# Eight batches of attention and FFN on one core: the last rotation, the block sums, the last contexts and bn_aggr moved

## The reference

```python
q = _rmsnorm(q_in @ wq_a.T) ; q = (q @ wq_b.T)          # 384 latent columns, 16 heads of 128 + 64
kv = x @ wkv_a.T ; kv_c = _rmsnorm(kv[..., :128])       # 128 latent columns, 64 rotated ones shared by heads
scores = einsum(qf, kf) * SCALE ; attn = softmax(scores) # 512 x 512 for each head
out = einsum(attn, v) ; x = x + out @ wo.T
x = x + down((silu(LN(x) @ gate) * (LN(x) @ up)))       # 512 -> 1536 -> 512
```

## Time and profile before

| what | us |
|---|---|
| median of three runs | 2216.45 |
| lowest and highest run | 2216.08, 2217.67 |
| the profiled execution, its own time | 2217.94 |
| its span | 2216.1 |
| PE busy | 2183.9 |
| DVE busy | 1595.4 |
| POOL busy | 1361.4 |
| ACT busy | 1281.6 |

### The profile page before, as it was taken

The page is one execution under the profiler, slowest core; times in us unless marked ns, Lnnn a source line. Parts: engine busy times, 40 slices in busy tenths (PEclk is TensorE's granted clock), DMA queues, the critical chain, the costliest instruction groups (busy, mean ns, idle before and its releaser), DMA issues.

```text
span 2216.1 us, 37420 instructions
## 1 busy us (share of the span) xinstructions
PE 2183.9 (99%) x11732; PEld 1100.9 (50%) x11732; DVE 1595.4 (72%) x3581; ACT 1281.6 (58%) x2688; POOL 1361.4 (61%) x1083
## 2 busy tenths in 40 slices
PE   7999999999999999999999999999999999999999
PEld 5444544445445564455644555445654556445554
DVE  7888886877567775777767777677766777467773
ACT  6666564554377732877328763487434874367722
POOL 4657466785378833887249772588536874368732
PEclk9999999999999999999999999999999999999999
DMA  7868436775158841788318882188723896148730
GB/s 247 190 124 151 91 72 149 153 149 119 29 127 160 163 96 22 147 163 167 77 32 158 164 155 65 41 169 161 142 55 64 167 165 127 27 98 157 148 82 20
DMA packets 734362, 265.44 MB, mean 120 GB/s; under 512 B 687312, under 2 KB 703696, under 8 KB 733136
## 3 DMA queue, kind: packets, MB, share of 16 engines
q1 hardware_dynamic: 734160, 263.05, 57.6%
HBM read 79.31 MB, written 14.81 MB: 42 GB/s over the span
## 4 chain that ended last, share of the span: by engine, by line
PE 85%; DVE 7%; POOL 2%; DMA 2%; ACT 2%; SPq 1%; issue 1%; DVEq 0%; ACTq 0%; POOLq 0%
PE bank L1108 13%; PE bank L921 8%; PE scores L1118 7%; PE bank L349 6%; PE bank L351 6%; PE bank L350 6%; PE scores L813 5%; PE scores L351 5%; PE scores L350 5%; PE scores L349 5%; PE bank L832 4%; PE bank L834 4%; PE bank L833 4%; PE scores L810 3%; DVE arena L1803 2%
## 5 line engine op out<-in xcount | busy, mean ns | idle before, releaser
L1774 DVE TENSOR_REDUCE mx<-scores 128x1 f32<-128x512 f32 x512 | 353.3, 690 | 62.7 <-PE scores L351 62.3
L2306 POOL TENSOR_TENSOR arena<-arena 128x1024 f16<-128x1024 f32 x168 | 354.3, 2131 | 38.2 <-ACT arena L1365 38.2
L1349 ACT ACTIVATE arena<-scores,shift 128x512 f32<-128x512 f32 x336 | 229.6, 686 | 148.5 <-DVE shift L1776 104.6
L1108 PE MATMUL bank<-arena,WFF 128*128 128x512 f16 x1392 | 313.5, 379 | 0.8 <-DVE arena L2099 0.6
L1858 DVE SCALAR_TENSOR_TENSOR arena<-bank,arena 128x512 f32<-128x512 f32 x336 | 216.8, 687 | 76.3 <-PE bank L921 75.5
L2405 POOL TENSOR_TENSOR arena<-arena 128x512 f16<-128x512 f32 x96 | 115.1, 1199 | 248.7 <-ACT arena L1491 248.7
L2221 POOL TENSOR_TENSOR arena<-arena 128x1024 f16<-128x1024 f32 x88 | 187.7, 2138 | 95.6 <-ACT arena L1339 95.4
L1108 PEld LDWEIGHTS bank<-arena,WFF 128*128 128x128 f16 x1392 | 136.0, 98 | 164.1 <-DVE arena L2099 2.3
L921 PE MATMUL bank<-WVO 128*128 128x256 f16 x1764 | 213.5, 273 | 0.3 <-DVE arena L1858 0.3
L813 PE MATMUL scores<-arena 128*128 128x512 f16 x512 | 195.4, 382 | 0.0
L921 PEld LDWEIGHTS bank<-WVO 128*128 128x128 f16 x1764 | 172.1, 98 | 46.1 <-DVE arena L1858 1.3
(11 more groups left out here) (198 smaller groups left out, 4699.8 us busy)
## 6 DMA issues: line engine op xcount, KB each, us to landing
WVO<-w_duo SPq DMA_DIRECT2D x42, 512.0 KB, 4.4
WVO<-w_duo SPq DMA_DIRECT2D x42, 384.0 KB, 3.9
arena<-arena SPq DMA_TRANSPOSE x712, 3.3
arena<-w_ffn SPq DMA_DIRECT2D x24, 384.0 KB, 3.5
arena<-x SPq DMA_DIRECT2D x8, 1024.0 KB, 5.7
out<-arena SPq DMA_DIRECT2D x32, 256.0 KB, 2.0
arena<-x SPq DMA_DIRECT2D x14, 512.0 KB, 4.6
WVO<-w_o SPq DMA_DIRECT2D x4, 1024.0 KB, 8.4
```

The lines of the kernel that those rows point to most:

```text
L1108: m = pe.matmul(dst[:, :], lhsT=w[:, c, k, :], rhs=XT[:, p, k, :], start=(k == 0 and p == 0), stop=(k == NK - 1 and p == 1))
L1774: dve.tensor_reduce(mx[:, t:t + 1], SC[:, t, :], AX_X, ALU.max).then_inc(s["mxr"], 1)
L2306: pool.tensor_tensor(PL[:, par, two, :], exps(i)[:, two, :], PH[:, par, two, :], ALU.subtract).then_inc(s["pl"], 1)
```

## The change

- **Rotation 7.** In batches 0 and 1 PE issues it behind scores(1), DVE takes it up behind the maxima of head 1, and in batch 1 POOL's part follows accordingly.
- **Transposes of head 0.** SP issues hi0, hi1, lo0, lo1 instead of hi0, lo0, hi1, lo1, in plain and duo batches.
- **Block sums (batch 1).** `block_sums(j, 0)` makes the first six steps in the even head, `block_sums(j, 1)` the other four in the next one; the low halves, ACT's high halves and SP's sums of blocks come one head later, and the rows of the next batch in heads 7, 9 and 11.
- **The last contexts.** For batches 1 to 7 ACT makes the high halves of the context of head 14 and of both halves of head 15 in the new `end_context_hi`, DVE only the low halves. `end_context_hi` waits for `outp` besides `ctp` and `cth`.
- **bn_aggr.** In batches 0 to 6 three of the four come between the third and the fourth bn_stats.
- **Batch 7.** The context of head 14 is one full operation, the second half's low part comes directly behind `stats(1)`, and `keep_warm(8)` becomes `keep_warm(4)`.

```diff
+        ROWS_PLAIN = {7: (0,), 9: (1, 2), 11: (3,)}
...
                 prob_rows_hi(g, par, 0)
+                if i == 0:
+                    prob_rows_hi(g, par, 1)
                 prob_rows_lo(g, par, 0)
-                prob_rows_hi(g, par, 1)
+                if i > 0:
+                    prob_rows_hi(g, par, 1)
                 prob_rows_lo(g, par, 1)
...
+                if i == 0:
+                    prob_rows_hi(b * NH, 0, 0)
+                    prob_rows_hi(b * NH, 0, 1)
+                    prob_rows_lo(b * NH, 0, 0)
+                    prob_rows_lo(b * NH, 0, 1)
+                    return
...
-                        if i >= 4 and i % 2 == 0:
-                            sums_of_blocks(i // 2 - 2)
+                        if i >= 5 and i % 2:
+                            sums_of_blocks((i - 5) // 2)
...
                 scores(b, pair, par)
+                if rot is not None:
+                    rotated_ahead(b, rot)
...
-                for n in range(rot_first(first) + 1, N_ROT):
-                    rotated_ahead(b, n)
+                    rotated_ahead(b, N_ROT - 1)
+                elif first:
+                    rotated_ahead(b, N_ROT - 2)
...
-                    head_step(b, 0, 1)
+                    head_step(b, 0, 1, rot=N_ROT - 1)
...
-                    keep_warm(8, SC[:, 2])
+                    keep_warm(4, SC[:, 2])
...
+            def end_context_hi(n, cols, src, read, parts=1):
+
+                act.wait_ge(s["ctp"], n + parts)
+                act.wait_ge(s["cth"], n)
+                act.wait_ge(s["outp"], read)
+                act.activation(CT[:, 0, cols], src[:, cols], ACT.Copy, scale=CS).then_inc(s["cth"], parts)
...
+                        if i >= 4 and i % 2 == 0:
+                            sum_hi(i // 2 - 2)
+                        for t in ROWS_PLAIN.get(i, ()):
+                            next_rows_hi(b, t)
...
+                    if plain and not first and k == 0:
+                        sum_hi(N_DUO - 2)
+                    if not first and k == 1:
+                        n, d = b * N_CT + 2 * N_DUO, order_of_head(b, 2 * N_DUO) if b >= B_PLAIN else (b * NH + NH - 2) * NT
+                        end_context_hi(n, slice(0, S), BQ, d, 2 if last else 1)
...
+                    for half in range(2):
+                        end_context_hi(n + 2 + half, half_cols(half), VBANK_END[1][half], d + 2 + 2 * half)
                     x_hi(b + 1)
                     return
-                for i in range(2, 2 * NT - 2):
+                latent(b + 1, 2)
+                if not first and plain:
+                    end_context_hi(n + 1, half_cols(0), VBANK_LAST[0], d + 2)
+                latent(b + 1, 3)
+                if not first and not plain:
+                    end_context_hi(n + 1, half_cols(0), VBANK_LATE[0], d + 2)
+                if not first:
+                    end_context_hi(n + 2, half_cols(1), (VBANK_LAST if plain else VBANK_LATE)[1], d + 4)
+                for i in range(4, 2 * NT - 2):
...
-            def context(n, cols, src=BC):
-
-                dve.wait_ge(s["ctp"], n + 1)
-                dve.tensor_scalar(CT[:, 0, cols], src[:, cols], CS, None, ALU.mult).then_inc(s["cth"], 1)
-                dve.wait_ge(s["cth"], n + 1)
-                split_lo(CT[:, 1, cols], src[:, cols], CS, CT[:, 0, cols]).then_inc(s["ctl"], 1)
+            def context(n, cols, src=BC, hi=True, parts=1):
+
+                if hi:
+                    dve.wait_ge(s["ctp"], n + 1)
+                    dve.tensor_scalar(CT[:, 0, cols], src[:, cols], CS, None, ALU.mult).then_inc(s["cth"], 1)
+                dve.wait_ge(s["cth"], n + parts)
+                split_lo(CT[:, 1, cols], src[:, cols], CS, CT[:, 0, cols]).then_inc(s["ctl"], parts)
...
+                if turned is not None:
+                    rot_products(b, turned, RBANK[turned % 2])
                 sums_of_head(g - 1, 1 - par)
+                if row is not None:
+                    next_rows(b, row)
...
-                dve.wait_ge(s["ctp"], n + 1)
-                for half in range(2):
-                    context(n - 1 + half, cols[half], BQ)
+                context(n - 1, slice(0, S), BQ, hi=False, parts=2)
...
                 stats(0)
                 stats(1)
+                context(n + 2, cols[1], VBANK_END[1][1], hi=False)
                 add_last(b, 7, 6)
-                context(n + 2, cols[1], VBANK_END[1][1])
                 norm(0)
...
-                context(n - 1, slice(0, S), BQ)
+                context(n - 1, slice(0, S), BQ, hi=first)
...
+                    if t == NT - 2:
+                        ch.wait()
+                        for k in range(NT - 1):
+                            ch.add(dve.bn_aggr(mv[:, k, :], bn[:, k, :]))
+                ch.add(dve.memset(rs_t[:, 0:NT], 0.0))
                 ch.wait()
-                ch.add(dve.memset(rs_t[:, 0:NT], 0.0))
-                for t in range(NT):
-                    ch.add(dve.bn_aggr(mv[:, t, :], bn[:, t, :]))
+                ch.add(dve.bn_aggr(mv[:, NT - 1, :], bn[:, NT - 1, :]))
...
+                if part == 1:
+                    step(t2, half(o, 0, 1), t1, ALU.subtract, 3)
+                    step(t2, t2, half(o, 1, 1), ALU.add, 7)
+                    step(t4, half(o, 0, 0), t2, ALU.subtract, 8)
+                    step(t4, t4, half(o, 1, 0), ALU.add, 9)
+                    return
...
-                step(t2, half(o, 0, 1), t1, ALU.subtract, 3)
-                step(t2, t2, half(o, 1, 1), ALU.add, 7)
-                step(t4, half(o, 0, 0), t2, ALU.subtract, 8)
-                step(t4, t4, half(o, 1, 0), ALU.add, 9)
...
-                        if i % 2 == 0:
-                            block_sums(i // 2 - 1)
-                        else:
-                            block_sums_lo(i // 2 - 1)
+                        j = i // 2 - 1
+                        if i % 2 == 0 and j > 0:
+                            block_sums_lo(j - 1)
+                        block_sums(j, i % 2)
...
+                if plain and not first:
+                    block_sums_lo(N_DUO - 1)
```

More of the change, by code:

```diff
@@ L300, in halves_landed, with half_cols @@
             return (b * (NH // 2) + i // 2) * 32
+        def half_cols(half):
+            return slice(2 * half * P, 2 * half * P + 2 * P)
         def any_bank(n):
@@ L597, in batch @@
                         next_input(b)
-                    if plain and i in (11, 12):
+                    if first and i in (11, 12):
                         turn_input(b, i - 11, stg)
+                    elif plain and i == 12:
+                        turn_input(b, 0, stg)
+                        turn_input(b, 1, stg)
                     if not plain and not last and i in TURN_STEPS:
@@ L978, in before, with head_step @@
                 return (pair, 0) if par else (pair - 1, 1)
-            def head_step(b, pair, par, first=False, ahead=True, weights=False):
+            def head_step(b, pair, par, first=False, ahead=True, weights=False, rot=None):
                 if weights:
@@ L1892, in duo_step, with head_step @@
                     duo_adds(b, (i - 5) // 2, (4, 5, 6, 7))
-            def head_step(i, b, par, ahead=True, chunk=None, part=None, weights=False, rot=None):
+            def head_step(i, b, par, ahead=True, chunk=None, part=None, weights=False, rot=None, turned=None, row=None):
                 g, n = b * NH + i, b * N_CT + i
@@ L1951, in attention @@
                     head_step(i, b, i % 2, chunk=chunk_of(i) if first else None, part=part,
-                              weights=first, rot=N_ROT - 1 if first and i == 2 else None)
-                    if not first and 7 <= i < 7 + NT:
-                        next_rows(b, i - 7)
+                              weights=first, rot=N_ROT - 1 if first and i == 2 else None,
+                              row=i - 7 if not first and 7 <= i < 7 + NT else None)
             def end_of_attention(b):
@@ L2004, in end_of_attention @@
                 duo_adds(b, N_DUO - 1, (0,))
-                context(n + 1, cols[0], VBANK_END[1][0])
+                context(n + 1, cols[0], VBANK_END[1][0], hi=False)
                 duo_adds(b, N_DUO - 1, (1, 2, 3))
@@ L2066, in last_of_attention @@
                 half_context = lambda half: context(n + half, slice(2 * half * P, 2 * half * P + 2 * P),
-                                                    (VBANK_LAST if b < B_PLAIN else VBANK_LATE)[half])
+                                                    (VBANK_LAST if b < B_PLAIN else VBANK_LATE)[half], hi=first)
                 if b >= B_PLAIN:
@@ L2254, in next_rows_lo, with block_sums @@
                 pool.tensor_tensor(STG[:, 1, t, :], XN[:, t, :], STG[:, 0, t, :], ALU.subtract).then_inc(s["xs"], 1)
-            def block_sums(j):
+            def block_sums(j, part):
                 k, e, o = 10 * j, WVO[:, 2 * j], WVO[:, 2 * j + 1]
@@ L2386, in attention @@
                         join_chunk(chunk_of(i - 1))
```

(12 more changed lines are left out.)

13 lines of the change are left out of this document (4 added, 9 removed).

## The result

The changed kernel takes 2223.68 us (median of eight runs, 2221.72 to 2225.64) against 2216.55 (eight runs, 2215.91 to 2217.67): ratio 1.0029, 95% interval 1.0020 to 1.0039. It is slower, by 4.4 to 8.6 us; 2217.4 had been forecast, with a range that ended at 2221.4. The forecast was 0.9 us above the median before; the measured step is 7.1. The profiled execution took 2222.42 us with a span of 2220.6, against 2217.94 and 2216.1 before, so the two traces explain 4.5 us.

What follows compares the result with a forecast made beforehand. PE, busy 99%, was taken as the bound, with some 11 us of waits to win. Terms +4.5, +1.5, -1.6, -1.6, -1.75 made +1.0 on 2217.94, so 2218.9, less 1.5 to the median: 2217.4, range 2211.8 to 2221.4.

Steps and rivals of the forecast that it cites:

- The gate: Head 14's context, batches 2 to 6: ACT's high half waits for `outp` after the sixth pair's products; +4.5 us in all.
- the slack: Before head 14's projection, batch 3: DVE's second add ended 1.11 us before PE needed it.
- next_rows: hidden: Next batch's rows, moved earlier in DVE heads 7 to 10 and POOL and ACT heads 7, 9, 11: 0 us.
- bn_aggr: Layer norm, batches 0 to 6: three aggregations ahead of the last bn_stats add one dependent drain; +0.2 us each, +1.5.
- Rival 2: Layer norm: early bn_aggr is free, since DVE holds the next operation anyway; -1.5 us, giving 2215.9; chance 0.13.
- Block sums: Batch 1: ten steps split over even and odd heads bring transposes sooner, removing PE's waits; -1.6 us.
- the order of the transposes: Head 0 of batches 2, 3 and 6: hi1 ahead of lo0 lands lo1 earlier, removing PE's waits; -1.6 us.
- The rotation: Rotation 7 behind scores(1), batches 0 and 1: the wait moves into the scores, values(0) starts as before; 0 us.
- Batch 7: Last batch: earlier projection and norm, four fewer warming products, second transposes earlier; -1.75 us.
- rival 4: Batch 7: clock still 0.50 at the transposes and gate products, up to 4.2 us more, 2221.6; chance 0.16.

Runs made afterwards that it cites:

- Experiment 2: Changed kernel, but in duo batches ACT's high half of head 14's context waits for `outp` only at the batch-start count: 2217.90 us, ratio 0.9999.
- experiment 7: Version of experiment 4 with the duo batches' `outp` wait set two counts below the full one: 2214.14 us, ratio 0.9984.
- Experiment 1: Changed kernel with DVE's next_rows of heads 7 to 10 of batch 1 behind the additions again: 2221.17 us, ratio 1.0014.
- experiment 5: Changed kernel with next_rows as scalar_tensor_tensor with a broadcast scale, at the same new place: 2224.59 us, ratio 1.0028.
- experiment 8: Kernel before plus only the two-part block sums, with their POOL, ACT and SP parts: 2216.42 us, ratio 0.9994.
- experiment 4: Changed kernel with three repairs: next_rows behind the additions, weak `outp` wait in duo batches, four bn_aggr together again: 2213.39 us, ratio 0.9980.
- experiment 6: Version of experiment 4 with the last rotation back ahead of head 1's scores in batches 0 and 1: 2213.02 us, ratio 0.9980.

## Why the prediction was wrong

Its sum was +1.0 us on the profiled execution; the traces say +4.5, the medians +7.1.

**The gate was right in place and nearly in size.** Forecast +0.8 and +0.1 a batch, measured 0.88 and 0.20; the additions 1.93 us later were 1.86 later, and the second addition was what PE waited for. Experiment 2 takes it away, experiment 7 finds no price inside the slack. What was mis-sized is the last batch: +0.2 was named for the gate there, and left out of the sum, and 1.1 came back when it was weakened.

**The step that failed is "next_rows: hidden".** I reasoned that DVE is busy 72% of the span and waits for PE before each context, took the operation to be as short at the new place as elsewhere, and gave it 0 us. It cost 2.23, in three waits of 0.72 to 0.77. Two things were missed. The new place is, within some hundredths of a us, the moment at which POOL starts the split of a head's probabilities, since both follow ACT's last exponential. And this DVE operation, when it begins while POOL works, ends 0.28 us behind the end of an operation of POOL: so in all nine of its executions of this kind in the trace before and in all seven after. The trace of before already showed it, where the wait was covered; POOL, then DVE:

```profile
458.42 2.13 POOL L2286 TENSOR_TENSOR WVO<-arena,WVO 128x1024 f16<-128x1024 f32 x1
...
458.59 0.68 DVE L1562 SCALAR_TENSOR_TENSOR arena<-bank,arena 128x512 f16<-128x512 f32 x1
459.19 1.65 DVE L1676 TENSOR_SCALAR arena<-arena,mv,rs_x 128x512 f32<-128x512 f32 x1
```

Inside POOL's 2.13 us an operation that reads a bank took its usual 0.68 us; the row operation behind it, which reads and writes float32 in SBUF, began at 459.19 and ended at 460.84, 0.29 behind POOL's end. In the trace before, the four executions in heads 7 to 10 of batch 1 took 1.05, 1.00, 1.65 and 0.79 us: all four were held, where it cost PE nothing. A look at the spread of this line (0.537 us at least, 0.543 in the middle, 1.646 at most) would have raised the question. Experiment 1 shows the price, experiment 5 that another form of the operation is held too.

**bn_aggr was right in sign, a third too dear.** Forecast +0.2 seven times, measured 0.15. Rival 2, by which a wait costs DVE nothing, fell: the longer chain is seen in PE's wait.

**Block sums and the order of the transposes.** Forecast -1.6 and -1.6. In batch 1 the waits went as said (experiment 8: -1.25 net), and the one at the start of batch 2 is gone from every trace with the new order. The split sums may have made that wait longer first (experiment 8), so the two terms may not be independent. But batch 5 shows a wait of 0.73 us for transposed probabilities ahead of values(2) (PE at 1464.67) that the trace before lacks. Such waits stand in other batches from trace to trace, one to four idle times of over 0.1 us in batches 1 to 7 of each kernel with the new order, all one or two heads behind the batch's first values. The load of the batch's rows goes out between the transposes shortly before (SP at 1453.27 in this trace); whether it is the cause isn't shown. Laid beside the undisturbed batch 4 of experiment 4, PE's starts in batches 2 to 6 lose 1.8 us at values(0) before (2.8 in experiment 8) and nothing in the eight traces with the new order; ahead of values(2) they lose 0.1 us with the old order and 0.4 to 2.1 with the new one, 0.9 in the changed kernel. So the forecast 1.6 was won where it was sought, and from a quarter of it to more than all was lost again two heads later. The order alone wasn't run, so what makes the later waits stays open; between the two traces, batch 2 shows 0.9 less than the price of gate and bn_aggr, batch 6 some 0.5 less, batch 5 some 0.7 more.

**The rotation: right**, 0 in batch 1, with the wait of 1.47 us turned into 0.86 and 0.18 within the scores; experiment 6 confirms it.

**Batch 7: near in size, partly by luck.** Forecast -1.75 and +0.2, measured -1.2: the gate cost 0.9 more, and without it the batch takes 268.9 instead of 271.2 us, a gain of 2.3, not of 1.75. The clock did what neither the forecast nor rival 4 had said. The forecast had the four warming products at half clock, 1.65 us, and rival 4 had the clock down for longer; it didn't fall at all, and the four took 1.03 us. With an idle stretch of 0.98 us ahead of the projection it stayed at 1.00 in all eight traces that have the new end, and it was 0.50 for 3.41 us in both that have the old one, with 2.3 us idle there. The mean clock of a run without a trace can't tell this: it is below 1.000 in 28 of 32 and in 20 of 30 runs of the kernel before and in one of eight of the changed one, but also in one to five of eleven runs of the repaired versions, and a fall in the last microseconds of the span, which most traces show, lowers it as well. The number of products and the length of the stretch changed together, so which of them keeps the clock isn't shown.

**The last step, from the profiled execution to the median, rested on too little.** I took off 1.5 us because that execution was 1.5 above the median of three runs, as if the changed kernel's would be too. It was 1.3 below its own: 4.5 between the traces, 1.4 and 1.3 on either side of them make the 7.1 between the medians. In two further sets of runs the kernel before had medians of 2217.46 (32 runs) and 2217.74 (30 runs), near the profiled execution. Against those, the changed kernel would be 6 us slower. The profiled executions of the experiments lie from 1.5 us below to 1.6 above the median of their own kernel, so the gap between 4.5 and these 6 or 7 us is within what one execution scatters; the small total of waits for transposes in the changed kernel's trace (1.4 us, 2.1 to 3.5 in the six others) points the same way. The changed kernel wasn't timed again, and the interval of the ratio (4.4 to 8.6) holds all three.

By batch, the traces differ from the forecast's terms by about 3.2 us: batch 1 by 2.3 (next_rows), batch 5 by 0.7 and batch 3 by 0.3 (waits for transposes), batch 7 by 0.3, the start and the others by -0.4 together.

## What to carry to other kernels

- Before a small DVE operation is moved, look at what POOL does at the new moment, and at each execution of that line, not at its usual length. Here all four of the moved ones had been held by POOL before, for up to 1.65 us and under cover; at the new place both engines follow the same event and started within 0.02 us of each other in three of four heads, and there the hold has its full length, 2.4 us, and no cover.
- A semaphore count that stands for "this tile has been read" often counts more than that. Moving the operation to another engine with such a wait moves the later of the two conditions onto its chain; ask for the lowest count that is enough. Here that was worth 6.5 us by the traces.
- A delay costs about what it exceeds the slack by (0.87 us for 1.86 with a slack of 1.11, nothing for 0.55); a sum for a change should start from that slack. And a profiled execution isn't moved to the median by three runs.

The version with the three repairs (experiment 4) beats both kernels: 2213.39 us, ratio 0.9980.

## What the runs showed of the hardware

- The row operation of DVE (TENSOR_SCALAR, reads float32 from SBUF and writes float32 to SBUF, 512 columns) took 0.52 to 0.55 us where POOL hadn't begun. Begun 0.01 us behind POOL's subtraction of 1024 columns it took 2.40; begun 0.07 us ahead of it, 0.52, and POOL's took 2.44 instead of 2.13. In these traces one of the two stands until the other is done, and the one that began clearly first goes first; with DVE ahead by only 0.02 us (head 10) it was DVE that was held.
- A small operation can be held as well. The softmax sum of a plain head has 4 columns and takes 0.16 us; where it began while POOL worked (14 of 44) it took 0.24 to 2.10 in the changed kernel. Operations on one column (L1817, 348 of them begun while POOL worked) took 0.15 us throughout; why they escape isn't shown:

```profile
L1822 DVE TENSOR_SCALAR dsum<-esum x44: 157/160/2102, 73.2 to 2138.4; 128x4 f32<-128x4 f32 x44
```

- Reading float32 from SBUF is not enough to be held: 23 of these 28 operations, `bn_stats` of the next batch's rows, began while POOL worked, and none took over 0.70 us:

```profile
L1701 DVE BATCH_NORM_STATS2 bn<-arena x28: 662/677/695, 110.2 to 1636.4; 128x6 f32<-128x512 f32 x28
```

- Operations that read a bank were not held. Those of `add_out` (bank and SBUF to SBUF) have 0.731 us at least and 0.753 at most in the changed kernel, over 172 of them, 104 of which began while POOL worked; the row operation there has 0.518 and 2.425:

```profile
L1845 DVE SCALAR_TENSOR_TENSOR arena<-bank,rden,arena x172: 731/742/753, 77.5 to 2134.8; 128x512 f32<-128x512 f32 x172
```

```profile
L1717 DVE TENSOR_SCALAR arena<-arena,mv,rs_x x24: 518/540/2425, 430.4 to 1688.9; 128x512 f32<-128x512 f32 x24
```

- Whether the row operation 0.3 us earlier, ahead of the softmax sums, would win against the split in each head wasn't tried.
